# Self-attention's softmax in a Perceiver block: exponentials head by head on ScalarE, with the negated maximum as bias and the sums from the accumulator

## The reference

```
x = x + _L0_attn_ref(_layernorm(x), w_attn, b_attn, w_proj, b_proj)

qkv = x @ w_attn + b_attn                                 # split into q, k, v; 16 heads of 32
att = jnp.einsum('bhqd,bhkd->bhqk', q, k) * hd ** (-0.5)
att = jnp.where(causal[None, None], att, -jnp.inf)
att = jax.nn.softmax(att, axis=-1)
out = jnp.einsum('bhqk,bhkd->bhqd', att, v)
return out @ w_proj + b_proj
```

## Time and profile before

| | |
|---|---|
| median of 3 runs | 1532.4 us (1530.95 to 1535.75) |
| profiled execution, its own time | 1530.84 us |
| its span, first to last instruction | 1528.7 us |
| mean granted TensorE clock | 0.995 |
| TensorE, VectorE, ScalarE, GpSimd busy | 97%, 81%, 64%, 11% |
| self-attention's softmax, first to last instruction on `sc` | about 1367.9 to 1407.8 us |

### The profile page before, as it was taken

How to read it: one execution, slowest core, us unless ns; L and a number is a source line. 1 busy time by engine, 2 the same in 40 slices (tenths; PEclk the granted TensorE clock), 3 DMA queues, 4 the chain that set the end, 5 groups by cost and what they waited for, 6 DMA issues and landing times.

```text
span 1528.7 us, 22000 instructions
## 1 busy us (share of the span) xinstructions
PE 1480.6 (97%) x6890; PEld 1195.9 (78%) x6926; DVE 1242.1 (81%) x1944; ACT 978.0 (64%) x3657; POOL 163.3 (11%) x120
## 2 busy tenths in 40 slices
PE   6989999999999999999999999999999998998898
PEld 5767777888888888888888888888888877886787
DVE  6657778988988889898889988998898999768443
ACT  4565667766776667677666766776677666634332
POOL 2210000002000200020002002000200211023242
PEclk9999999999999999999999999999999999999999
DMA  5532221211221122112111211121011143650000
GB/s 179 176 104 79 70 69 42 67 54 31 76 62 41 42 72 67 35 59 62 56 45 55 62 52 45 56 62 45 25 60 40 45 144 99 225 221 1 1 1 28
DMA packets 86467, 105.20 MB, mean 69 GB/s; under 512 B 7240, under 2 KB 67664, under 8 KB 85328
## 3 DMA queue, kind: packets, MB, share of 16 engines
q1 hardware_dynamic: 79056, 96.46, 20.3%
q10 hardware_dynamic: 7296, 7.34, 1.5%
HBM read 81.24 MB, written 22.54 MB: 68 GB/s over the span
## 4 chain that ended last, share of the span: by engine, by line
PE 76%; DVE 15%; ACT 4%; issue 3%; DMA 1%; POOL 0%; another core or an unknown queue 0%; ACTq 0%; DVEq 0%; POOLq 0%
PE ps L36 24%; PE ps L37 23%; PE ps L38 23%; DVE ring L1086 3%; PE ps L859 2%; PE ps L860 2%; DVE p_lo L42 1%; ACT ps L1609 1%; DVE ring L1057 1%; PE ps L877 1%; PE ps L878 1%; DVE run_max L1077 1%; DVE k_sum L1030 1%; DVE q_rstd L987 0%; DMA wq_raw<-in_wq 0%
## 5 line engine op out<-in xcount | busy, mean ns | idle before, releaser
L1609 ACT ACTIVATE ps<-ps 123x128 f32<-123x128 f32 (+1 forms) x1248 | 325.2, 261 | 135.2 <-PE ps L38 134.6
L36 PE MATMUL ps<-wk_hi,cT_hi 128*128 128x512 f32 x832 | 329.5, 396 | 8.0 <-ACT ps L1609 5.0
L37 PE MATMUL ps<-wk_lo,cT_hi 128*128 128x512 f32 x832 | 326.0, 392 | 0.0
L38 PE MATMUL ps<-wk_hi,cT_lo 128*128 128x512 f32 x832 | 323.9, 389 | 0.0
L1609 ACT ACTIVATION_READ_ACCUMULATOR ps<-ps 123x1 f32 (+1 forms) x1248 | 231.0, 185 | 0.0
L36 PEld LDWEIGHTS ps<-wk_hi,cT_hi 128*128 128x128 f32 x832 | 156.1, 188 | 51.2 <-ACT ps L1609 10.9
L38 PEld LDWEIGHTS ps<-wk_hi,cT_lo 128*128 128x128 f32 x832 | 156.3, 188 | 34.4
L37 PEld LDWEIGHTS ps<-wk_lo,cT_hi 128*128 128x128 f32 x832 | 156.7, 188 | 31.6
L36 PE MATMUL ps<-p_hi,cn_hi 123*128 123x512 f32 (+1 forms) x400 | 164.7, 412 | 0.0
L36 PE MATMUL ps<-fq_hi,cT_hi 128*128 128x512 f32 x416 | 162.2, 390 | 1.9 <-DVE fq_lo L42 1.9
L37 PE MATMUL ps<-fq_lo,cT_hi 128*128 128x512 f32 x416 | 161.9, 389 | 0.0
(11 more groups left out here) (235 smaller groups left out, 2693.8 us busy)
## 6 DMA issues: line engine op xcount, KB each, us to landing
cT_raw<-in_ctxT SPq DMA_DIRECT2D x96, 128.0 KB, 3.5
cn_raw<-in_ctx SPq DMA_DIRECT2D x88, 123.0 KB
w_raw<-in_wguT SPq DMA_DIRECT2D x32, 256.0 KB, 2.7
qk_scratch<-folded ACTq DMA_DIRECT2D x8, 896.0 KB, 4.2
fq_raw<-qk_scratch SPq DMA_DIRECT2D x14, 512.0 KB, 3.8
pc_scratch<-pc_out SPq DMA_DIRECT2D x7, 1024.0 KB, 4.2
ternary_scratch<-w_out SPq DMA_DIRECT2D x48, 128.0 KB, 1.7
w_bf<-ternary_scratch SPq DMA_DIRECT2D x1, 6144.0 KB, 22.8
```

The source lines that it names most:

```text
L36: pe.matmul(dst, l_hi, r_hi, start=first, stop=False)
L37: pe.matmul(dst, l_hi, r_lo, start=False, stop=False)
L38: return pe.matmul(dst, l_lo, r_hi, start=False, stop=last)
L1609: done = act.activation(head, head, ACT.Square, accum_out=k_sum[0:n, i, g * GH + h:g * GH + h + 1])
```

## The change

In `causal_shifted` the subtraction over 128 x 1024 goes; in its place the 128 x 16 maxima are negated in place. `causal_exp` now runs head by head: 16 exponentials over 64 columns each, with the head's negated maximum as bias (a column of numbers, one for each partition) and its sum put out by the accumulator. `causal_probs` loses its sum over 128 x 1024 and the wait behind it. Each semaphore is raised as often as before, by the last instruction of its step; `causal_sum` is gone.

```diff
@@ causal_shifted, causal_probs (VectorE)
                 dve.wait_ge(causal_max, m + 1)
-                dve.tensor_tensor(sc[:, i], sc[:, i], row_max[:, i].unsqueeze(2).broadcast_to([P, SH, TQ]),
-                                  ALU.subtract).then_inc(causal_shift, 1)
+                dve.tensor_scalar(row_max[:, i], row_max[:, i], -1.0, None, ALU.mult).then_inc(causal_shift, 1)
 
             def causal_probs(m):
                 i, hp = m % 2, slice(0, TQ)
                 dve.wait_ge(causal_exped, m + 1)
-                dve.tensor_reduce(row_scale[:, i], sc[:, i], AX_X, ALU.add).then_inc(causal_sum, 1)
-                dve.wait_ge(causal_sum, m + 1)
                 dve.reciprocal(row_scale[:, i], row_scale[:, i]).then_inc(causal_rec, 1)
@@ causal_exp (ScalarE)
             def causal_exp(m):
                 act.wait_ge(causal_shift, m + 1)
-                act.activation(sc[:, m % 2], sc[:, m % 2], ACT.Exp).then_inc(causal_exped, 1)
+                for h in range(SH):
+                    row = sc[:, m % 2, h]
+                    done = act.activation(row, row, ACT.Exp, bias=row_max[:, m % 2, h:h + 1],
+                                          accum_out=row_scale[:, m % 2, h:h + 1])
+                done.then_inc(causal_exped, 1)
```

More of the change, by code:

```diff
@@ L359, in perceiver_block @@
             sem("causal_mm"), sem("causal_scaled"), sem("causal_max"), sem("causal_shift"), sem("causal_exped"))
-        causal_sum, causal_rec, diag_top, diag_low = (
-            sem("causal_sum"), sem("causal_rec"), sem("diag_top"), sem("diag_low"))
+        causal_rec, diag_top, diag_low = (
+            sem("causal_rec"), sem("diag_top"), sem("diag_low"))
         pT_turned, pT_copied, attend_mm = sem("pT_turned"), sem("pT_copied"), sem("attend_mm")
```

## The result

The changed kernel took 1537.88 us in the median of 7 runs (1537.04 to 1540.11), against 1532.4 before (1530.95 to 1535.75, 7 runs of that comparison): ratio 1.0035, 95% interval 1.0023 to 1.0047. It is slower by 5.5 us, clear of the 0.3% only by its middle, not by its interval. The forecast was 1543 us, with a range of 1539 to 1548.

What follows compares the result with a forecast made beforehand. TensorE held 76% of the last chain, but in self-attention the others wait for VectorE from the third tile's scores. 1530.84 + 10.2 (path) + 0.5 (clock) = 1541.5, or 1543.1 against the median; range 1539 to 1548.

Steps and rivals of the forecast that it cites:

- The path: Self-attention: all four tiles' exponential groups lie on the critical chain, moving tile 0's cast of attended values by +10.2 us.
- The price of the pair: ScalarE: one 64-column exponential plus its accumulator read costs 0.36 us, bounds 0.27 and 0.53; sixteen take 5.76 us.
- The twin in the earlier trace: Key squares on ScalarE: ACTIVATE 0.27 us, read 0.18, next pair after 0.28, so the read hides but for 0.01 to 0.02.
- The clock term: TensorE's granted clock falls again after longer waits ahead of tiles 0 and 1: +0.5 us, bounds 0 and 2.
- A second fall: TensorE's clock falls perhaps twice, the first after a wait of about 3 us ahead of tile 0, behind ScalarE's copies.
- the one from the profiled execution to the medians: Whole execution: the median lies 1.6 us above the profiled 1530.84, so 1541.5 became 1543.1 against the median.
- the hold-up: VectorE's low parts and GpSimd's probabilities at tile 0 slow each other; rival that this falls away: 1541.7 us, chance 0.06.
- the first rival: Not slower: ScalarE has room and VectorE's relief wins; 0.03 faster, 0.05 within 0.3%; a 0.27 us pair gives +4.4, 1537.
- One named sign of being wrong: In the changed profile, a low clock in the feed-forward that comes or goes; no size given.
- The rival of equal speed: Self-attention on ScalarE: shift is nil at 0.20 us per pair, faster only below; chance 0.05 within 0.3%, 0.03 faster.

Runs made afterwards that it cites:

- the doubled pairs: Changed kernel with each head's exponential cut into two of 32 columns, each with bias and accumulator; 1558.78 us, ratio 1.0187 to the kernel before.
- the other three: Three more comparisons of the unaltered changed kernel with the unaltered kernel before: ratios 1.0063, 1.0064 and 1.0059.
- sums alone: Changed kernel's sixteen exponentials with accumulator but no bias, VectorE subtracting as before; 1537.33 us, ratio 1.0044 to the kernel before.
- bias alone: Changed kernel's sixteen exponentials with the negated maximum as bias but no accumulator, VectorE summing again; 1535.45 us, ratio 1.0027 to the kernel before.
- exponential 3 late: Changed kernel with tile 3's sixteen exponentials moved behind tile 1's probability copies in ScalarE's queue; 1538.17 us, ratio 1.0054 to the kernel before.
- tile 2 alone: Kernel before with the three changed steps taken for tile 2 only; 1527.75 us, ratio 0.9983 to the kernel before.

## Why the prediction was right or wrong

**The path was right, event by event.** The sum did not come close by luck. With 0.60 us taken off the times after for the later start, the probabilities of tile 0 are at 1377.06 (forecast 1377.56), scores of tile 1 at 1382.32 (1382.83), probabilities of tile 1 at 1390.96 (1391.95), scores of tile 2 at 1392.70 (1393.70), copies of tile 0 at 1400.93 (1402.39), the fourth group at 1404.02 (1405.52), the cast at 1409.33 (1411.28). All four groups lie on the path, and the doubled pairs confirm it.

**The price of the pair was mis-sized, 0.36 us forecast, 0.333 measured.** Times 64 that is 1.8 of the 1.95 us by which the cast came earlier than forecast. Two parts: an ACTIVATE of 0.335 instead of 0.345, and a read that adds nothing over the ACTIVATE's own duration instead of 0.015. The twin in the earlier trace rows misled me: I carried its excess over from 128 columns of PSUM to 64 of SBUF. The Trainium skill, "ScalarE: Activation LUTs", section "What ACT_TABLE_LOAD costs", gave 333 ns for the ACTIVATE and, with the rows' read, 0.33 for the pair; the measurement agrees with the page, and its 93 ns for a pointer operand is the 0.09 found here.

**The clock term, +0.5, was not there.** B is the same with and without the change in the first profiles. TensorE's wait ahead of tile 1's attention did grow from 2.40 to 4.81 us and the clock did fall behind it, but by no more than before: 0.83 over the ten us from 1399 before and from 1407 after. A second fall, within the three stretches below, followed a wait of 1.87 us for the weights' low parts and not, as forecast, the wait ahead of tile 0's attention. It did not show in the path: the scores of tile 2 came at 1392.70, earlier than forecast.

```profile
1383.06 0.50 PE L36 MATMUL ps<-wa_hi,yT_hi 128*128 128x512 f32 x1 [1.87 <-DVE wa_lo L42]
...
1411.03 0.66 PE L776 MATMUL ps<-pT,v_nat 128*32 128x128 f32 x8 [4.81 <-ACT pT L1860]
```

```profile
1382.00:1384.00 2.00, 0.94 (x3) 0.79 (x4) 2.00 (x6) 0.00 (x0) 0.00 (x0) 0.91 0.00 0
1384.00:1386.00 2.00, 2.00 (x6) 1.59 (x5) 1.72 (x3) 0.18 (x1) 0.00 (x0) 0.50 0.00 0
1386.00:1388.00 2.00, 2.00 (x42) 1.34 (x41) 0.29 (x1) 2.00 (x13) 0.00 (x0) 0.73 0.00 0
```

**The step that failed is the one from the profiled execution to the medians.** The forecast of 1543.1 stood 5.2 us above the measured 1537.88. The path accounts for 1.95 of them (1.8 by the pair), the clock term for 0.5, and 2.8 are left. I gave the scatter no term, without a reason: I moved the profile's 1530.84 up to the median by 1.6 and took the changed kernel to lie as high over its own profile, while its median came out 1.4 below. The low end of the range was drawn by the pair's price and the hold-up alone. With the 8.3 us that A shows, 1532.4 would have become 1540.7, inside the range; with a pair of 0.36 us on the same runs it would have been 1537.88 + 1.8 = 1539.7, also inside. So it took both, the mis-sized pair and the untreated scatter, and the scatter is the larger. Why this comparison lies 3 to 4.5 us below the other three is open.

The 1537 that the first rival gives for a pair of 0.27 us lies near the measured time by coincidence: the pair took 0.333, and A grew by 8.3 and not by 4.4. One named sign of being wrong did show, a low stretch in the feed-forward that comes and goes, worth 1.4 us in B.

**The other steps.** The hold-up between VectorE and GpSimd stayed: the four low parts took 4.20 us before and after, and GpSimd's first half of the probabilities 3.54 before and 4.14 after. The low parts before, and GpSimd's row after:

```profile
1375.63 4.20 DVE L42 TENSOR_TENSOR wa_lo<-wa_raw,wa_hi 128x512 fp32r<-128x512 f32 x4
```

```profile
1377.70 4.14 POOL L1993 TENSOR_TENSOR p_diag<-sc,row_scale 64x1024 f32<-64x1024 f32 x1 [9.86 <-DVE row_scale L1390]
```

So the rival in which it falls away is out in this order of starts, as the rule of the Trainium skill, "SBUF — State Buffer", section "SBUF: two separate sides", said. The rival of equal speed needed 0.20 us a pair; sums alone or bias alone stand at 0.24 and still lose.

## What to carry to other kernels

Cutting one wide ACTIVATE into heads pays a fixed price each time: here 0.33 us for 64 columns with bias and sum, sixteen for 5.3 us, to save 1.06 us on ScalarE and 2.2 on VectorE. Price the pieces by their start-to-start distance, then ask in whose queue they stand: the same group alone cost 3.3 us of A at tile 3 and nothing at tile 2. And look at what stands behind a waiting step in its queue before changing the step: moving one exponential behind copies that did not need it gave 2.3 us on the path for one edited line.

## What the runs showed of the hardware that was not expected

A low stretch of TensorE's clock costs by where it falls. From 1384 to 1388 in the changed kernel, while VectorE and ScalarE held the path, nothing was seen of it; in tile 1's output projection, with exponential 3 late, it took back the 2.65 us gained. And a kernel whose distance A was unchanged (tile 2 alone) ran 2.6 us faster, with the low stretches in its attention and at the start of its feed-forward gone in its profile. The distance A, by contrast, repeated within 0.02 us over seven profiles, while whole executions lay up to 4.1 us from their median and one comparison of the medians missed the other three by 3 us or more: for a change of half a percent, the distance between marked instructions was the surer measure.
